# A decoder layer on one core: step tables moved to GpSimd, row-number scatters and bias adds moved in its queue, another order at both ends of the last FFN stage

## The reference

```python
x = x + attn(layernorm(x))    # linear attention, 16 heads of 32
x = x + moe(layernorm(x))     # 4 experts by token number; Wg = Wu = Wd = ctx_2048
x = x + ffn(layernorm(x))     # ternary weights, 512 -> 2048 -> 512

# attn: q = k = elu(x @ Wqk + bqk); v = silu(x @ Wv + bv); u = silu(x @ Wu + bu)
#       kv = sum_n k^T v per head; o = layernorm(q @ kv) * ln_g + ln_b
#       result (u * o) @ Wo + bo
# moe:  e = min(id // 6250, 3); h = silu(x @ W[e].T) * (x @ W[e].T); y = h @ W[e].T
# ffn:  w -> clip(round(w / mean|w|), -1, 1) * mean|w|
#       result (silu(x @ Wu.T) * (x @ Wg.T)) @ Wd.T
```

## Time and profile before

| what | value |
| --- | --- |
| median of 3 runs | 765.36 us |
| the profiled execution's own time | 763.66 us |
| its span on the core | 761.9 us |
| PE busy | 715.7 us (94%) |
| DVE busy | 386.8 us (51%) |
| ACT busy | 273.1 us (36%) |
| POOL busy | 131.0 us (17%) |
| mean granted TensorE clock | 0.988 of full |

### The profile page before, as it was taken

The page is one execution under the profiler, slowest core; times in us unless marked ns, Lnnn a source line. Parts: engine busy times, 40 slices in busy tenths (PEclk is TensorE's granted clock), DMA queues, the critical chain, the costliest instruction groups (busy, mean ns, idle before and its releaser), DMA issues.

```text
span 761.9 us, 11591 instructions
## 1 busy us (share of the span) xinstructions
PE 715.7 (94%) x3948; PEld 381.1 (50%) x3978; DVE 386.8 (51%) x655; ACT 273.1 (36%) x426; POOL 131.0 (17%) x171
## 2 busy tenths in 40 slices
PE   8998999899899869999998999999999999999993
PEld 6565457457446546666554444444444444444441
DVE  5669766846836746655465333343334333342232
ACT  4365545536436334454322332222222222222220
POOL 4202124404606840000010000020001100020002
PEclk9999999999999999999999999999999999999998
DMA  8924026006207369650102000020001100010001
GB/s 238 343 72 149 1 101 208 23 8 216 108 1 275 126 199 390 240 153 29 29 15 42 15 14 11 4 69 15 14 14 25 58 14 14 15 55 1 0 0 55
DMA packets 48182, 63.99 MB, mean 84 GB/s; under 512 B 25360, under 2 KB 25360, under 8 KB 47120
## 3 DMA queue, kind: packets, MB, share of 16 engines
q1 hardware_dynamic: 43792, 50.89, 21.0%
q0 software_dynamic: 4352, 12.60, 4.3%
HBM read 46.69 MB, written 12.59 MB: 78 GB/s over the span
## 4 chain that ended last, share of the span: by engine, by line
PE 82%; DVE 6%; POOL 4%; issue 3%; ACT 2%; SPq 1%; DMA 1%; DVEq 0%; ACTq 0%; POOLq 0%
PE bank L1342 29%; PE bank L1070 28%; PE bank L1352 14%; PE bank L1063 4%; PE bank L1263 3%; PE bank L1227 2%; DVE late L759 1%; POOL sorted_ids L330 1%; PE bank L1241 1%; POOL sorted_tokens L322 1%; DMA stage<-in_L_attn_Wv_dram 1%; DVE region L606 1%; POOL sorted_residual L326 1%; SPq L190 1%; DVE st L598 1%
## 5 line engine op out<-in xcount | busy, mean ns | idle before, releaser
L1342 PE MATMUL bank<-w_att,region 128*128 128x512 f16 (+1 forms) x1024 | 231.3, 379 | 1.0 <-issue 1.0
L1342 PEld LDWEIGHTS bank<-w_att,region 128*128 (+1 forms) x1024 | 100.1, 98 | 122.0 <-issue 1.5
L1036 DVE SCALAR_TENSOR_TENSOR tmp<-tmp,hk,bank 128x512 f32<-128x512 f32 x64 | 47.8, 747 | 161.6 <-PE bank L1342 161.1
L1352 PE MATMUL bank<-region,tmpA 128*128 (+1 forms) x474 | 116.9, 379 | 1.6
L309 POOL TENSOR_SCALAR ve<-mv 128x1 f32<-128x1 f32 (+1 forms) x37 | 9.5, 256 | 485.0 <-DVE mv L974 336.2
L1070 PE MATMUL bank<-late,w_att 128*128 128x512 f16 x384 | 86.1, 379 | 4.0 <-DVE region L806 3.9
L575 ACT ACTIVATE tmp<-bank,qs 128x512 f32<-128x512 f32 x64 | 44.0, 687 | 122.4 <-PE bank L1342 122.4
L579 ACT ACTIVATE tmpA<-tmp 128x512 f16<-128x512 f32 x64 | 40.3, 629 | 121.5 <-DVE tmp L1036 121.5
L1352 PEld LDWEIGHTS bank<-region,tmpA 128*128 128x128 f16 x504 | 49.2, 98 | 59.6 <-DVE stage L1020 0.9
L1039 DVE TENSOR_TENSOR tmpA<-tmp,tmpA 128x512 f16<-128x512 f32 x64 | 44.4, 693 | 45.6 <-ACT tmpA L579 45.6
L1070 PEld LDWEIGHTS bank<-late,w_att 128*128 128x128 f16 x384 | 37.2, 98 | 46.4 <-DVE region L806 4.7
(11 more groups left out here) (143 smaller groups left out, 813.1 us busy)
## 6 DMA issues: line engine op xcount, KB each, us to landing
stage<-in_L_ffn_W_up_dram SPq DMA_DIRECT2D x8, 1024.0 KB, 5.4
stage<-in_L_ffn_W_gate_dram SPq DMA_DIRECT2D x8, 1024.0 KB, 5.5
stage<-in_ctx_dram SPq DMA_DIRECT2D x4, 1024.0 KB, 6.4
stage<-in_L_ffn_W_down_dram SPq DMA_DIRECT2D x4, 1024.0 KB, 7.3
nrm<-in_L_ffn_W_down_dram SPq DMA_DIRECT2D x4, 1024.0 KB, 7.8
n<-sorted_tokens SPq DMA_DIRECT2D x16, 256.0 KB, 4.2
resid<-sorted_residual SPq DMA_DIRECT2D x4, 1024.0 KB, 9.3
resid<-in_x_dram SPq DMA_DIRECT2D x1, 3072.0 KB, 19.0
```

Of the source, the lines that this page charges most:

```text
L1036: dve.scalar_tensor_tensor(out=h32, in0=sil, scalar=hk[:, 0:1], in1=gate_ps[:, :], op0=ALU.mult, op1=ALU.mult).then_inc(s["hid_mul"], 1)
L1342: mm = pe.matmul(dst, w[:, bass.ds(cf_c, 1), k * P:(k + 1) * P].rearrange("p a n -> p (a n)"), x3T[:, bass.ds(b, 1), i, k].rearrange("p a ...
L1352: mm = pe.matmul(ffy_ps[t][:, :], hid[:, parity, i, t * P:(t + 1) * P], tern[2][:, bass.ds(c, 1)].rearrange("p a n -> p (a n)"), start=(st ...
```

## The change

Five edits.

1. The step tables are made by POOL, behind the square roots of batch 0's attention output (`step_tables`), each instruction with a wait for the one before. Their scratch moves to the weight store of the last expert, so ACT waits for the tables before it writes that store in batch 3. DVE's `gated_mul` now waits for the positions alone. The rounding down to a multiple of 128 is replaced by a comparison with a bound (`last`).
2. The 16 row-number scatters go behind the last residual scatter on POOL, and SP's load of the row numbers behind its last sorted tile.
3. POOL's bias adds of batch b wait for `v_bias(b, 0)`.
4. In the last group of the last FFN batch, the downs of chunks 12 to 14 are left out of the chunk loop and made together with that of chunk 15, tile by tile; chunks 14 and 15 go to another buffer (`hid_late`). The second product of the last expert step stands behind the first up product of the FFN, and the waits for that step stand later.
5. `keep_busy` between the first two weight units makes 100 products for 70.

```diff
-    sv = region[:, 5, 2, 0:10 * STEPS].rearrange("p (i j) -> p i j", j=STEPS)
+    sv = w_moe[:, E - 1, 0, 0].bitcast(F32)[:, 0:9 * STEPS].rearrange("p (i j) -> p i j", j=STEPS)
+    hid_late = n2[:, 0:2].rearrange("p a d -> p (a d)").bitcast(F16).rearrange("p (i h n) -> p i h n", i=2, h=2)
...
# SP
-        sp.wait_ge(s["id_sent"], 16 * NT)
-        sp.dma_start(row_id[:, :], id_v, allow_slow_non_contiguous=True).then_inc(s["id_in"], 16)
         for i in range(9, NT):
             sp.wait_ge(s["tx_mm"], i - 2)
             sorted_tile(i)
+
+        sp.wait_ge(s["id_sent"], 16 * NT)
+        sp.dma_start(row_id[:, :], id_v, allow_slow_non_contiguous=True).then_inc(s["id_in"], 16)
...
# POOL
         def batch(b):
             pool.wait_ge(s["x_norm"], T * b + T)
+            pool.wait_ge(s["v_bias"], T * b + 1)
             for t in range(T):
                 pool.tensor_tensor(resid[:, T * b + t], resid[:, T * b + t], bo_bc[:, :], ALU.add).then_inc(s["bias_added"], 1)
...
-            if 0 < b < B - 1:
+            if b == 0:
+                step_tables()
+            elif b < B - 1:
                 scatter_residual(b - 1)
-                scatter_ids(b - 1)
+        def made_by(ins):
+
+            made[0] += 1
+            ins.then_inc(s["steps_made"], 1)
+            pool.wait_ge(s["steps_made"], made[0])
+
+        def step_tables():
+
+            pool.wait_ge(s["route_pos"], 1)
+            pool.wait_ge(s["starts_made"], 3)
...
+            for e in range(1, E):
+                made_by(pool.tensor_scalar(last[:, e:e + 1], base[:, e:e + 1], float(NT * P - 1), float(P * e - P + 1),
+                                           ALU.min, ALU.add))
...
         scatter_residual(B - 2)
-        scatter_ids(B - 2)
-        scatter_ids(B - 1)
         rsqrt_tile(2, "x2_aggr", T * (B - 1), 0, "rs2_last")
...
         scatter_residual(B - 1)
+        for b in range(B):
+            scatter_ids(b)
...
# ACT
-                if not (first and cc < 2):
+                if not (first and cc < 2) and not (ends and cc >= 2):
                     act.wait_ge(s["down_mm"], cf - 1)
-                act.activation(hid[:, cc % 2, 0], h32, ACT.Copy).then_inc(s["hid_hi"], 1)
+                if first and cc == 1:
+                    act.wait_ge(s["y_mm"], STEPS)
+                dst = hid_late if ends and cc >= 2 else hid
+                act.activation(dst[:, cc % 2, 0], h32, ACT.Copy).then_inc(s["hid_hi"], 1)
...
# DVE
             if first:
                 routing_positions()
-                routing_steps()
...
# PE
-        keep_busy(ps[3], 70)
+        keep_busy(ps[3], 100)
...
-        second(STEPS - 1)
...
                 two_pass(up_ps[:, :], tern[0], c, b).then_inc(s["up_mm"], 1)
+                if begin:
+                    second(STEPS - 1)
...
-                else:
-                    if begins and cc == 1 and not first:
-                        pe.wait_ge(s["out_made"], T * b)
+                elif not (ends and cc > 0):
+                    if begins and cc == 1:
+                        if first:
+                            pe.wait_ge(s["y_evac"], STEPS)
+                        else:
+                            pe.wait_ge(s["out_made"], T * b)
                     down(cf - 1, c - 1, (cc - 1) % 2, begins and cc == 1, False)
         pe.wait_ge(s["unit_copy"], 12 * T)
-        pe.wait_ge(s["y_evac"], STEPS)
         pe.wait_ge(s["x3_in"], 16 * T)
...
-        for i in range(2):
-            pe.wait_ge(s["hid_lo" if i else "hid_hi"], C * B)
-            for t in range(T):
-                mm = pe.matmul(ffy_ps[t][:, :], hid[:, 1, i, t * P:(t + 1) * P], tern[2][:, C - 1],
-                               start=False, stop=(i == 1))
-                if i == 1:
-                    mm.then_inc(s["down_last"], 1)
+        for t in range(T):
+            for cc in range(4):
+                src = hid if cc < 2 else hid_late
+                for i in range(2):
+                    if t == 0:
+                        pe.wait_ge(s["hid_lo" if i else "hid_hi"], C * B - 3 + cc)
+                    mm = pe.matmul(ffy_ps[t][:, :], src[:, cc % 2, i, t * P:(t + 1) * P], tern[2][:, C - 4 + cc],
+                                   start=False, stop=(cc == 3 and i == 1))
+            mm.then_inc(s["down_last"], 1)
```

More of the change, by code:

```diff
@@ L106, in decoder @@
     tokf = sb("tokf", [P, NT])
-    pad_i = sb("pad_i", [P, 2, E], I32)
-    pad_f = sb("pad_f", [P, 2, E])
+    last = sb("last", [P, E])
     base = sb("base", [P, E])
@@ L161, in decoder @@
         w_hi w_lo ctx_mm ctx_hi ctx_lo abs_done abs_mm scale_step
-        route_step route_mm route_read route_ready
+        route_step route_pos steps_made route_mm route_read route_ready
         x_stat x_aggr x_norm t1_mm x_hi x_lo
@@ L444, in batch @@
             else:
+                if last:
+                    act.wait_ge(s["route_ready"], 3)
                 ctx_hi(b, 0)
@@ L568, in _, with group @@
             expert_step(i)
-        def group(b, t, first, nxt):
+        def group(b, t, first, nxt, ends=False):
             for cc in range(4):
@@ L584, in batch3 @@
             group(b, 0, first, nxt)
-            with act.Fori(1, T) as t:
+            with act.Fori(1, T if nxt else T - 1) as t:
                 group(b, t, False, nxt)
-        act.wait_ge(s["y_mm"], STEPS)
+            if not nxt:
+                group(b, T - 1, False, False, True)
         batch3(0, True, True)
@@ L727, in first_tile @@
+            dve.tensor_copy(pos[:, :], pos_f[:, :]).then_inc(s["route_pos"], 1)
         def first_tile(t):
@@ L750, in gated_mul @@
             if k == 0:
-                dve.wait_ge(s["route_ready"], 3)
+                dve.wait_ge(s["route_pos"], 1)
             if last:
@@ L1021, in finish, with group @@
                                          in1=x_tile(T * b + t), op0=ALU.mult, op1=ALU.add).then_inc(s["out_made"], 1)
-        def group(b, t, begins, first, nxt):
+        def group(b, t, begins, first, nxt, ends=False):
             for cc in range(4):
@@ L1038, in group @@
                 dve.wait_ge(s["hid_hi"], cf + 1)
-                dve.tensor_tensor(hid[:, cc % 2, 1], h32, hid[:, cc % 2, 0], ALU.subtract).then_inc(s["hid_lo"], 1)
+                dst = hid_late if ends and cc >= 2 else hid
+                dve.tensor_tensor(dst[:, cc % 2, 1], h32, dst[:, cc % 2, 0], ALU.subtract).then_inc(s["hid_lo"], 1)
                 if nxt and cc == 2:
@@ L1044, in batch3 @@
             group(b, 0, True, first, nxt)
-            with dve.Fori(1, T) as t:
+            with dve.Fori(1, T if nxt else T - 1) as t:
                 group(b, t, False, False, nxt)
+            if not nxt:
+                group(b, T - 1, False, False, False, True)
             if not first:
@@ L1382, in batch3 @@
             group(b, 0, True, first, nxt)
-            with pe.Fori(1, T) as t:
+            with pe.Fori(1, T if nxt else T - 1) as t:
                 group(b, t, False, False, nxt)
+            if not nxt:
+                group(b, T - 1, False, False, False, True)
         batch3(0, True, True)
```

60 lines of the change are left out of this document (24 added, 36 removed).

## The result

The changed kernel takes 773.14 us (median of 4 runs, 772.51 to 773.62) beside 765.51 us of the kernel before on the same chip (764.87 to 767.97): the ratio is 1.0093, with a 95% interval of 1.007 to 1.0117. The forecast was 753.0, faster. The profiled execution took 772.51 us with a span of 770.8 and a mean granted clock of 0.979.

The account below looks back on a forecast made before the run. The chain was 82% PE, so time is won only where PE idles or is slowed. Gains of 2.9 + 2.6 + 4.4 + 0.4 + 2.1 = 12.4 us took the 765.36 median to 753.0, range 748.0 to 758.0.

Parts of the forecast that it names:

- Row-number scatters and keep_busy: Between the first two weight units: earlier statistics and 100 filling products win 4.4 us, bounds 3.1 to 5.5.
- Rival 3: Expert stage can't start 4.4 us earlier because the loads shift by only 3.1: 754.3 us, chance 0.06.
- Rival 4: Batch 1: the step tables' chain on POOL starves DVE at `gated_mul` 0; slower, 774.8 or 763.9 us, chance 0.04.
- Step tables, 2.9: Batch 1: tables off DVE win 2.02 us at the q clips and 0.86 at the head norm, bounds 0 to 3.2.
- Bias adds held, 2.6: Batches 1 to 3: `gated_mul` 2 held for a whole train, PE idles 2.5 us each; gain 2.6, bounds -2.6 to 10.1.
- Rival 1: DVE gets in between bias adds, only late steps late by some 1.2 us a batch: 749.1 us, chance 0.2.
- Rival 2: The clock falls in each of the three 2.5 us stalls, costing 3 x 1.75 = 5.25: 758.2 us, chance 0.15.
- the price of no clock loss: Value stage, batches 1 to 3: the 24 products behind each 2.5 us idle keep full speed, so 0 us priced.
- The adds of batch 0, priced at nothing: Batch 0: adds move to DVE work with a PSUM input, worth nothing, or up to 0.8 us per clip.
- Seam, 4.4: Between weight units (0,0) and (0,1): work 3.1 us earlier and full clock worth 1.35 more, 4.4 us in all.
- FFN's start, 0.4: FFN's start: first up product may start earlier, 32 products end at 424.0 for 424.4; bounds 0 to 2.5.
- End, 2.1: Last FFN batch: two downs leave the last gate's way, last scatter at 751.2 or 751.3 for 753.4; bounds 1 to 3.

Follow-up runs that it names:

- ids_late: Changed kernel with POOL waiting, ahead of the 16 row-number scatters, until PE has turned 11 blocks of sorted tiles: 749.55 us, ratio 0.9803.
- ids_64B: Changed kernel, scatters at the same place, each row number written as the first word of a 64-byte row: 750.56 us, ratio 0.9809.
- only_ids: Kernel before with only the row-number scatters moved behind the last residual scatters and their load behind the last sorted tile: 785.1 us, ratio 1.025.
- the twelve shifted trains: Four kernels on ids_late with 1 to 26 POOL memsets between value bias and bias adds in batches 1 to 3: 749.04, 751.61, 752.44, 750.24 us.
- late_nohold: ids_late without POOL's wait for the first value bias ahead of the bias adds: 760.52 us, ratio 0.9941.
- ids_back: Changed kernel with the 16 row-number scatters back behind the residual scatters of batches 0 to 2: 754.28 us, ratio 0.9859.

## Why the prediction was wrong

**The failed step** is in "Row-number scatters and keep_busy": "The 16 row numbers (20 us of POOL) now lie in the expert stage, where POOL has nothing else and SP asks for them after its last tile." It priced them by POOL's time and by who waits for them, and left out what they do to the queues they share. I had asked what the moved step issues on its own engine and queue, and not what it lies beside. By the times ids_late puts the price at 23.6 us and ids_64B at 22.6; by the ratios it is 22.2 and 21.7. In only_ids the expert stage alone loses 26 us by the rows, of which 20 are left in the time. Nothing in the rows of before showed it, since there the same scatters ran in the attention stage with few loads beside them (53 load packets of 0.30 MB while the last eight were issued, 250 to 263 us); but no row showed them beside a stream of loads either, so the step was an operation in a place that the trace did not show, and wanted a bound on the side of a loss. Rival 3 named the right stage (a wait for loads in the first steps) with another cause and a price of 1.3 us. Rival 4, the only slower one, had the wrong place: the tables' chain ran on POOL from 67.6 to 80.7 us, 13 us for my 11, and starved nobody.

**Step tables, 2.9:** right. PE idles 0.36 us ahead of the third q product and not at all for the head norm: 2.0 and 0.86 us by the rows. Undone alone, the times gave 2.7 and the ratios 1.4.

**Bias adds held, 2.6:** right in sign, undersized. The rows that answer to the earlier trace rows, PE in batches 1 to 3 of the changed kernel:

```profile
70.15 5.35 PE L1082 MATMUL bank<-late,w_att 128*128 128x512 f16 x24 [0.36 <-DVE region L816]
75.34 1.04 PE L1075 MATMUL bank<-ident,region 128*128 128x128 f32 x8
...
79.68 7.93 PE L1082 MATMUL bank<-w_att,late 128*128 128x512 f16 x36
88.76 10.52 PE L1082 MATMUL bank<-w_att,region 128*128 128x512 f16 x48 [0.71 <-DVE region L777]
...
146.12 10.52 PE L1082 MATMUL bank<-w_att,region 128*128 128x512 f16 x48 [0.66 <-DVE region L777]
...
203.42 10.52 PE L1082 MATMUL bank<-w_att,region 128*128 128x512 f16 x48 [0.67 <-DVE region L777]
```

Batches 2 and 3 take 4.28 and 4.36 us less from the third q product to the projection (18.56 for 22.84, 18.57 for 22.93), and batch 1 loses some 0.45: 8.2 for my 2.6. What failed is "I take that: `gated_mul` 2 ends at 146.8": the starving of the earlier trace rows was carried over to a train in another company. Rival 1, turns, was right, with `v_bias` 1 in time and the end of the row late, by 0.66 to 0.71 us a batch where it had 1.2; and the Trainium skill's rule ("SBUF — State Buffer", "Who interferes with whom": one instruction's length) holds in the twelve shifted trains and the changed kernel, where one instruction waits 1.1 us. It does not hold for trains behind a scatter, where four instructions pass. Rival 2 did not come up: PE had no such idle. But the row on which the price of no clock loss rested, 2.38 us of idle and the next 24 products at 5.35 us, can come out the other way. In only_ids the same place had 2.37 us of idle and a granted clock of 0.76 behind it (73.3 to 80.3 us):

```profile
73.33 7.04 PE L1070 MATMUL bank<-late,w_att 128*128 128x512 f16 x24 [2.37 <-DVE region L806]
```

The adds of batch 0, priced at nothing, were worth 0.12 us: PE reaches the products at 62.12 (62.79 before) 0.67 us earlier, 0.55 of which it is already ahead at 22.22. The 11 us of late_nohold measure something else than these 8.2: there the row numbers no longer stand ahead of the adds, and the head norm is held.

**Seam, 4.4:** right but for what it then caused. 4.08 us in the rows. POOL comes to the statistics at 246.7 and unit (0,1) runs at full clock behind 1.10 us of idle (0.7 forecast). Undone in two ways: the row numbers' place 4.7 us (ids_back against ids_late; 3.9 by the rows from unit (0,0) to the sorted transposes, 14.4 for 10.5), the 30 products 1.5 by their rows for my 1.35. That idle covers the 30 products was right by these rows.

**FFN's start, 0.4:** right by the rows, not run by itself. 32 products are through 12.3 us behind the step's transposes, for 12.8; an idle of 2.12 us takes the place of the two of the earlier trace rows.

**End, 2.1:** right within its bounds. From the expert stage's last transposes to the end of the last gate it is 3.1 us less (330.8 for 333.9), where the FFN's start and the two downs should give 0.5 + 3.45. Of the missing 0.85, 0.51 is a wait for a DMA transpose at 592.6 us, which the kernel before doesn't have; the rest was not located. The last scatter follows the gate by 8.87 us (753.41 to 762.28) for 7.9. Together both terms gave 2.1 us in the rows, where I had 2.5. The last four scatters stand 1.7 us apart, as said.

Put together, the five terms come to 765.5 - 749.55 = 16 us in ids_late (15.2 against the kernel before of the same hour, 764.75), where I had 12.4, and one uncounted cost of some 23 us turned them into a loss of 7.6. That the sum of the five came out near is partly luck: the hold gave 5.6 us more than its term, and ids_late's expert stage is 3.0 us longer than before, which no term had.

## What to carry to other kernels

When a DMA is moved, price it by what runs beside it at the new place, above all where the new place is the one stretch in which loads are late; "its engine is free there" is only half of the question. Index or flag scatters of a few bytes a row should be kept away from loads, or widened to 64 bytes a row, which took five edited lines here. Where DVE has work with two SBUF inputs or an f32 `tensor_scalar` on the path, keep long rows of GpSimd instructions from starting directly behind an indirect DMA; a wait between the two gave turns in every trace here.

## What the runs showed of the hardware

- 2048 rows of 4 bytes, written beside loads, stretched a packet of a load from 0.107 to 0.79 us and cost 20 to 24 us of an execution; 2048 rows of 64 bytes cost 0.9 to 2.4, which is not clear of noise, and of 2048 bytes 8.4 to 8.9. The same 4-byte scatters beside three tile loads that were not urgent slowed these (0.41 us a packet, up to 11.8 us to land for 2.5 to 2.8 before) and cost PE nothing (ids_late, 340 to 360 us).
- While loads were slow, the issue of a further one on SP took up to 11.62 us (0.3 to 0.5 is common), so a tile that was due later was asked for late as well.
- Four GpSimd adds gave DVE turns between them in most trains (6.6 us for a train in the changed kernel) and none in the seven trains directly behind an indirect DMA (4.92), where a `gated_mul` of 0.68 us took up to 5.64 and one of the head norm's instructions, 1.91 us for four in batch 1 of late_nohold, 5.70.
- A PE idle of 2.77 us between two weight units left the next at 3.59 us for 1.96 (granted clock 0.50). One of 2.38 in the attention stage was followed by full clock, and one of 2.37 at the same place in only_ids by 0.76, so the length of the idle alone did not decide it. After the idle of 23.35 us twelve products took 4.18 us for 2.76.
